# A two-layer residual block: rounding of the down weights on ScalarE and their later store, mask construction in batch 1's half, and other PSUM banks for the last pair

## The reference

```python
g = jnp.einsum('bsd,edf->ebsf', h, Wg)
u = jnp.einsum('bsd,edf->ebsf', h, Wu)
expert_outs = jnp.einsum('ebsf,efd->ebsd', jax.nn.silu(g) * u, Wd)
...
masked_scores = jnp.where(mask, scores[:, None, :], NEG_INF)
pooled = jnp.einsum('bjl,bld->bjd', softmax(masked_scores), hidden) / cnt[..., None]
```

## Time and profile before

| | us |
|---|---|
| runs | 1126.43, 1127.67, 1129.34; median 1127.67 |
| profiled execution | 1127.99 |
| its span, first to last instruction | 1126.1 |
| granted TensorE clock, mean | 0.995 |
| busy: PE, DVE, ACT, POOL | 1104.9, 919.6, 709.4, 696.5 |

### The profile page before, as it was taken

The page is one execution under the profiler, slowest core; times in us unless marked ns, Lnnn a source line. Parts: engine busy times, 40 slices in busy tenths (PEclk is TensorE's granted clock), DMA queues, the critical chain, the costliest instruction groups (busy, mean ns, idle before and its releaser), DMA issues. The chain is left out here.

```text
span 1126.1 us, 16076 instructions
## 1 busy us (share of the span) xinstructions
PE 1104.9 (98%) x4856; PEld 903.9 (80%) x4856; DVE 919.6 (82%) x1218; ACT 709.4 (63%) x1268; POOL 696.5 (62%) x666
## 2 busy tenths in 40 slices
PE   8799999999999999999999999999999999999988
PEld 6577888778888888888878887888888888888866
DVE  6698777788877877787668899888888898888875
ACT  6475666566666666666556666666666666666663
POOL 7799999999987777778324444444444444444451
PEclk9899999999999999999999999999999999999999
DMA  6666665487666666666545555555555555555512
GB/s 218 251 259 233 249 231 212 177 306 283 235 259 262 261 237 235 239 233 255 218 173 203 179 198 182 203 204 203 206 206 206 206 206 205 206 205 206 203 41 75
DMA packets 66484, 241.24 MB, mean 214 GB/s; under 512 B 6496, under 2 KB 38752, under 8 KB 57184
## 3 DMA queue, kind: packets, MB, share of 16 engines
q1 hardware_dynamic: 65584, 239.70, 57.6%
q10 hardware_dynamic: 816, 0.52, 0.2%
HBM read 134.29 MB, written 105.91 MB: 213 GB/s over the span
## 5 line engine op out<-in xcount | busy, mean ns | idle before, releaser
L811 ACT ACTIVATE silu<-g_ps 128x512 f32<-128x512 f32 x144 | 86.3, 599 | 180.1 <-PE g_ps L1480 180.1
L1478 PE MATMUL v_both<-xs_hi,wq 128*128 128x512 f32 x432 | 170.0, 393 | 3.3 <-DVE up L1146 2.6
L1479 PE MATMUL v_both<-xs_hi,wq 128*128 128x512 f32 x432 | 168.6, 390 | 0.0
L1480 PE MATMUL v_both<-xs_lo,wq 128*128 128x512 f32 x432 | 168.5, 390 | 0.0
L1141 DVE TENSOR_TENSOR gate<-e_ps,v_part 128x512 f32<-128x512 f32 x144 | 99.0, 687 | 66.4 <-PE e_ps L1480 66.2
L805 ACT ACTIVATE v_both<-g_ps 128x512 f32<-128x512 f32 x144 | 83.9, 583 | 101.7 <-PE g_ps L1480 101.4
L711 POOL TENSOR_TENSOR a<-a,a_own 128x512 f32<-128x512 f32 x35 | 56.1, 1604 | 137.4 <-DVE a_own L1173 137.4
L708 POOL TENSOR_TENSOR s<-a_own,a 128x512 f32<-128x512 f32 x35 | 56.3, 1610 | 131.0 <-DVE a_own L1192 131.0
L1478 PE MATMUL g_ps<-xs_hi,wq 128*128 128x512 f32 x288 | 113.0, 392 | 9.5 <-ACT v_both L805 9.5
L817 ACT ACTIVATE p_sb<-e_ps 128x512 f32<-128x512 f32 x144 | 86.2, 598 | 48.4 <-PE e_ps L1480 47.5
L1478 PE MATMUL e_ps<-xs_hi,wq 128*128 128x512 f32 x288 | 112.7, 391 | 0.4 <-ACT p_sb L817 0.4
(11 more groups left out here) (233 smaller groups left out, 2883.5 us busy)
## 6 DMA issues: line engine op xcount, KB each, us to landing
wq_kept<-wq SPq DMA_DIRECT2D x72, 896.0 KB, 5.5
wq<-wq_kept SPq DMA_DIRECT2D x72, 896.0 KB, 4.5
wd_kept<-wd SPq DMA_DIRECT2D x36, 1024.0 KB, 5.4
wd<-wd_kept SPq DMA_DIRECT2D x36, 1024.0 KB, 6.1
raw_d<-in_L_cond_Wd SPq DMA_DIRECT2D x32, 256.0 KB, 3.1
raw<-in_L_cond_Wg SPq DMA_DIRECT2D x31, 256.0 KB, 2.7
raw<-in_L_cond_Wu SPq DMA_DIRECT2D x31, 256.0 KB, 3.5
out_x<-x SPq DMA_DIRECT2D x8, 256.0 KB, 2.1
```

Source lines behind the costliest of these rows:

```text
L811: nc.scalar.activation(silu0[:, i % 2, :], g_ps[:], ACT.Silu).then_inc(silu0_done, 1)
L1478: nc.tensor.matmul(ps, w_hi, a_hi, start=start, stop=False, skip_group_check=True)
L1479: nc.tensor.matmul(ps, w_lo, a_hi, start=False, stop=False, skip_group_check=True)
L1480: return nc.tensor.matmul(ps, w_hi, a_lo, start=False, stop=stop, skip_group_check=True)
```

## The change

Eight things change in the code. (1) ScalarE gets `round_d(k)` at the end of even groups and `round_td(k)` at the end of odd ones, each one 128x512 copy; POOL keeps the lo parts (`rest_d`, `rest_td`) and `sums_d`, and of the old `split_d` only pair 0. (2) `raw_d` has three slots; SP loads pair 2 at n = 1. (3) `keep_d(k)`, the wait for `td_split`, the load of pair k+3 and the store of pair k, is moved from use 2k+1 to use 2k+6, so the last three lie in batch 1. (4) POOL makes the constants and masks in eleven parts, behind `sums_h(1)` to `sums_h(11)`. (5) `L1_AT` goes from 74 to 104; `add_acc(1)` of batch 0 stays at 74. (6) The last pair adds into `LAST`: `g_ps` and `v_ps[0]` for token half 0, `acc[0][1]` and `e_ps` for half 1; its first quarter stands ahead of `turn_sum(143)`. (7) VectorE's group 143 is written anew (`last_odd`), s3's drain goes to `p7_sb`, one of POOL's joins goes to VectorE. (8) ScalarE copies a11 to `res` ahead of `gate_second(143)`; batch 1's `attn` writes `acc[0][0]`.

```diff
+    RAWD = 3
...
+    KEEP = 3
...
-        raw_d = place("raw_d", [P, RAWS, DN, P], F32, work_at + 8 * BANK * 4)
+        raw_d = [place(f"raw_d{n}", [P, DN, P], F32, work_at + at * BANK * 4) for n, at in enumerate((8, 10, 25))]
...
-        L1_AT = end_of_b[0] + LAG + 1
+        ADD_AT = end_of_b[0] + LAG + 1
+        L1_AT = NU + 32
...
+        LAST = [[g_ps[:], v_ps[0]], [acc[0][1], e_ps[:]]]
+        ATT = [e_ps, acc[0][0]]
...
+            def keep_d(k):
+                sp.wait_ge(td_split, k + 1)
+                if k + RAWD < NU // PAIR:
+                    load_d(sp, k + RAWD)
+                sp.dma_start(wd_kept[k], wd[:, k % DR].bitcast(F32)).then_inc(wd_stored[k % DR], 16)
...
-                if n % PAIR == PAIR - 1:
-                    k = n // PAIR
-                    sp.wait_ge(td_split, k + 1)
-                    if m < NU // PAIR:
-                        load_d(sp, m)
-                    sp.dma_start(wd_kept[k], wd[:, k % DR].bitcast(F32)).then_inc(wd_stored[k % DR], 16)
+                if n == 1:
+                    load_d(sp, 2)
+                if n % PAIR == 0 and n // PAIR >= KEEP:
+                    keep_d(n // PAIR - KEEP)
...
+                k = i // PAIR - KEEP
+                if n % PAIR == 0 and k < NU // PAIR:
+                    keep_d(k)
...
             def split_d(n):
...
-                    pool.wait_ge(staged_d[s], (n // PAIR // RAWS + 1) * 16)
-                if n >= DR * PAIR:
-                    pool.wait_ge(down_done[1], n - DR * PAIR + 1)
-                    pool.wait_ge(wd_stored[n // PAIR % DR], n // PAIR // DR * 16)
-                k, own = n // PAIR % DR, slice(j * KD, (j + 1) * KD)
...
-                nc.gpsimd.tensor_tensor(hi, raw_d[:, s, own, :], zero[:, 0:1].unsqueeze(2).broadcast_to([P, KD, P]),
...
                                         ALU.add).then_inc(d_hi_done, 1)
                 pool.wait_ge(d_hi_done, n + 1)
-                nc.gpsimd.tensor_tensor(lo, raw_d[:, s, own, :], hi.bitcast(F32), ALU.subtract).then_inc(d_split, 1)
...
+            def rest_d(k):
+                own = slice(0, PAIR * KD)
+                pool.wait_ge(d_hi_done, PAIR + k)
+                nc.gpsimd.tensor_tensor(wd[:, k % DR, 1, own, :], raw_d[k % RAWD][:, own, :],
+                                        wd[:, k % DR, 0, own, :].bitcast(F32), ALU.subtract).then_inc(d_split, PAIR)
...
-                hi, lo = wd[:, k % DR, 0, 4:DN, :], wd[:, k % DR, 1, 4:DN, :]
-                nc.gpsimd.tensor_tensor(hi, w[:, 4:DN, :], zero[:, 0:1].unsqueeze(2).broadcast_to([P, DN - 4, P]),
-                                        ALU.add).then_inc(td_hi_done, 1)
+            def rest_td(k):
                 pool.wait_ge(td_hi_done, k + 1)
-                nc.gpsimd.tensor_tensor(lo, w[:, 4:DN, :], hi.bitcast(F32), ALU.subtract).then_inc(td_split, 1)
+                nc.gpsimd.tensor_tensor(wd[:, k % DR, 1, 4:DN, :], raw_d[k % RAWD][:, 4:DN, :],
+                                        wd[:, k % DR, 0, 4:DN, :].bitcast(F32), ALU.subtract).then_inc(td_split, 1)
...
-            EXTRA = {13: constants, 17: flags, 21: lambda: masks(0), 25: lambda: masks(1)}
...
-                if n in EXTRA:
-                    EXTRA[n]()
...
-                split_d(n)
+                if n < PAIR:
+                    split_d(n)
...
-                if n == 3:
-                    sums_d(0)
-                if n % PAIR and n > 1:
-                    sums_d(n // PAIR)
...
+                k = n // PAIR - 1
+                if n % PAIR == 0:
+                    if k >= 1:
+                        rest_d(k)
+                    if k >= 1:
+                        rest_td(k - 1)
+                elif k >= 0:
+                    sums_d(k)
+            last = NU // PAIR - 1
+            rest_d(last)
+            rest_td(last - 1)
+            sums_d(last)
+            rest_td(last)
...
                 joined_to(1, 0, xT[:, 1, 1, BANK:2 * BANK])
+                pool.wait_ge(res_step, 1)
+                joined_to(1, 0, res[:])
                 pool.wait_ge(res_step, 2)
-                joined_to(1, 0, res[:])
-                pool.wait_ge(res_step, 3)
-                joined_to(0, 1, res[:])
-                joined_to(1, 1, res[:])
+                joined_to(1, 1, p7_sb[:])
...
                     for p in range(SPS):
                         sums_h(p)
+                        if p in range(1, 12):
+                            pool.wait_ge(sum_made["s4"], p + 1)
+                        if p == 1:
+                            edges()
+                        elif p == 2:
+                            lanes()
+                        elif p == 3:
+                            blanks()
+                        elif p == 4:
...
+                        elif p in (6, 9):
+                            mask_of(p // 8)
+                        elif p in (7, 10):
+                            block_masks(p // 8)
+                        elif p in (8, 11):
+                            mask_ends(p // 11)
...
+            def round_d(k):
+                act.wait_ge(staged_d[k % RAWD], (k // RAWD + 1) * 16)
+                if k >= DR:
+                    act.wait_ge(down_done[1], (k - DR + 1) * PAIR)
+                    act.wait_ge(wd_stored[k % DR], k // DR * 16)
...
+                nc.scalar.activation(wd[:, k % DR, 0, own, :], raw_d[k % RAWD][:, own, :], ACT.Copy).then_inc(d_hi_done, 1)
+            def round_td(k):
+                act.wait_ge(td_step, 3 * (k + 1))
+                nc.scalar.activation(wd[:, k % DR, 0, 4:DN, :], raw_d[k % RAWD][:, 4:DN, :],
+                                     ACT.Copy).then_inc(td_hi_done, 1)
...
                     round_x(1, q)
+                if i % PAIR:
+                    round_td(i // PAIR)
+                elif i:
+                    round_d(i // PAIR)
...
                 if i + 1 < NG:
                     seed(i + 1)
-                gate_second(i)
                 if p == SPS:
                     act.wait_ge(c_used["a11"], SPS)
                     nc.scalar.activation(res[:], P_BANK["a11"], ACT.Copy).then_inc(p1_kept, 1)
+                gate_second(i)
...
-                    dve.wait_ge(joined, 2 * NT)
+                    dve.wait_ge(joined, 3)
+                    dve.wait_ge(res_step, 4)
...
                 for d in range(KD):
-                    nc.vector.tensor_tensor(xT[:, b, d, half], acc[d][t][:], xT[:, b, d, half],
+                    nc.vector.tensor_tensor(xT[:, b, d, half], LAST[t][d] if b else acc[d][t][:], xT[:, b, d, half],
...
-                if i == L1_AT:
+                if i == ADD_AT:
...
-                if p < SPS:
-                    rest_c("s3", p)
-                else:
-                    dve.wait_ge(p1_kept, 1)
-                    c11 = xT[:, 1, 0, 0:BANK]
-                    nc.vector.tensor_tensor(c11, P_BANK["a11"], c11, ALU.add).then_inc(res_step, 1)
-                    dve.wait_ge(c_used["s2"], SPS)
-                    nc.vector.tensor_tensor(res[:], P_BANK["s2"], res[:], ALU.add).then_inc(res_step, 1)
...
-                if p == SPS:
-                    dve.wait_ge(joined, NT)
-                    dve.wait_ge(res_step, 2)
-                    nc.vector.tensor_tensor(res[:], P_BANK["s3"], res[:], ALU.add).then_inc(res_step, 1)
...
+            def last_odd(i, p):
+                second_gate(i)
+                second_up(i)
+                hidden_second(i)
+                empty(i - 1)
+                dve.wait_ge(p1_kept, 1)
+                dve.wait_ge(c_used["s2"], SPS)
+                nc.vector.tensor_tensor(res[:], P_BANK["s2"], res[:], ALU.add).then_inc(res_step, 1)
+                hidden_first(i)
+                dve.wait_ge(c_used["s3"], SPS)
+                dve.wait_ge(res_step, 1)
+                nc.vector.tensor_tensor(p7_sb[:], P_BANK["s3"], res[:], ALU.add).then_inc(res_step, 1)
+                rest_c("a22", p)
+                rest_c("a12", p)
+                c11, c21 = xT[:, 1, 0, 0:BANK], xT[:, 1, 0, BANK:2 * BANK]
+                dve.wait_ge(c_used["a11"], SPS)
+                nc.vector.tensor_tensor(c11, P_BANK["a11"], c11, ALU.add).then_inc(res_step, 1)
+                dve.wait_ge(res_step, 2)
+                nc.vector.tensor_tensor(c21, c21, p7_sb[:], ALU.add).then_inc(res_step, 1)
+                dve.wait_ge(joined, 2)
+                empty(LAST_TURN)
+            for p in range(SPS):
                 even(NU + p * PAIR, p)
                 odd(NU + p * PAIR + 1, p)
-            empty(LAST_TURN)
+            even(NG - PAIR, SPS)
+            last_odd(NG - 1, SPS)
...
-            def last_pair():
...
-                        q = (("a11", "s3"), ("a12", "a22"))[f][t]
-                        if f == 0:
-                            pe.wait_ge(res_step, (3, 2)[t])
-                            down_sum(("a12", "a22")[t], SPS - 1, acc[0][t][:], True, False)
-                            if t:
-                                pe.wait_ge(emptied, LAST_TURN - FIRST_TURN + 1)
...
```

(73 more changed lines are left out.)

19 lines of the change are left out of this document (13 added, 6 removed).

## The result

| | before | after |
|---|---|---|
| median of 4 runs each, us | 1128.20 | 1118.28 |
| their range, us | 1126.43 to 1129.34 | 1117.90 to 1119.05 |
| ratio, 95% interval | | 0.9914, 0.9897 to 0.9931 |
| profiled execution / its span, us | 1127.99 / 1126.1 | 1118.34 / 1116.6 |

The change takes 9.9 us off the median, where 14.3 were forecast: faster by more than 0.3%, and inside the range by 0.3 us only, near its upper end. The kernel after is 4.6 us slower than the forecast's 1113.7, and the question of the experiments is where these went.

A forecast was written before the change was run, and what follows sets the result against it. TensorE was taken as the bound, with only its standing time to win. From 1127.99 us: -9.7 + 0 - 2.4 + 0.8 - 3.0 = -14.3, giving 1113.7 us; range 1109.8 to 1118.6.

The forecast's parts named there:

- The first hole: TensorE's pause at 38.53 to 46.70 us and the low clock behind it; SP's earlier store closes it, -9.7 us.
- the 1.4 of the term: Late `up`s in groups 5, 6 and 8 of batch 0; taken as 0, between -1.4 and +1.4 us.
- rival C: First hole only changes its owner, ScalarE being held as long in groups 1 to 4: 1123.4 or 1127 us; chance 0.10.
- The second hole: TensorE's waits behind masks(1) in batch 0, from about 204 us; they go when the masks leave, -2.4 us.
- ScalarE's and POOL's work in batch 0: ScalarE's added rounding copies fit its idle time and POOL only loses instructions; cost 0.
- 0.63 fits: 0: ScalarE's 0.63 us copy per group fits the 0.98 us idle ahead of the seed in batch 0; cost 0.
- rival A: VectorE's SBUF instructions collide with POOL's masks in eleven pairs of batch 1, 1.0 us a pair: 1123.9 us; chance 0.05.
- Masks in batch 1: Eleven mask parts behind s4 mostly fit POOL's idle time; the two mask_of make s3 late, +0.8 us.
- Rival B: POOL becomes the bound in batch 1, s3 and the seed late in eleven pairs: 1137 us, slower than before; chance 0.03.
- The end: Earlier up(143) and no wait ahead of the last pair, about 1090 us: -3.0 us.
- the masks' bound of 5.5 us: Upper bound for the masks in batch 1: eleven parts at 0.5 us each, in place of 0.8; sets the range's high end.

The follow-up runs named there:

- e4: Kernel before with only SP's new order (third raw_d slot, later keep_d): 1128.07 us, ratio 1.0000.
- e3: Kernel after with the rounding of the down weights (hi parts) given back from ScalarE to POOL: 1115.05 us, ratio 0.9881.
- e5: Kernel before with only the masks and constants moved to batch 1 and the second layer's steps at groups 104 to 118: 1126.35 us, ratio 0.9983.
- e1: Kernel after with one added wait: POOL starts rest_d only when VectorE has finished its rest_w: 1111.12 us, ratio 0.9846.
- e7: e1 with each of ScalarE's rounding copies made twice, the first into a spare tile: 1111.54 us, ratio 0.9855.
- e10: e1 run once more unchanged, for comparison on one chip with a version with split masks: 1110.86 us, ratio 0.9844.
- e6: Kernel before with only the new end (other banks, last_odd, first quarter ahead of the last turn): 1124.88 us, ratio 0.9972.
- e2: Kernel after with ScalarE's round_d and round_td moved into the next group, between gate_second and gate_first: 1117.81 us, ratio 0.9905.

## Why the prediction was right, and where it was not

**The first hole, -9.7: right.** Its gap and its low clock are gone, and after is 9.60 us ahead at group 5 and 9.98 at group 12; late `up`s of 0.38, 0.52 and 0.50 us stay in groups 3, 6 and 8, within the 1.4 of the term. But the prediction gave this gain to SP's order, and e4 shows that SP's order alone gives it back: rival C (the hole only changes owner) is what it does alone. What keeps the gain is not mainly ScalarE's rounding: e3, in which POOL rounds, still is 7.41 us ahead at groups 12 to 24, with the masks in batch 1 and POOL's steps in their new order. What each of these two does for the first groups, and ScalarE's rounding without SP's order, was not tried.

**The second hole, -2.4: right.** e5 measures 2.75. Before lost another 0.7 us in small places up to group 72, as e1 beside it shows, so 3.4 us came here.

**ScalarE's and POOL's work in batch 0, 0: the step that failed.** In the prediction: "0.63 fits: 0", and for POOL only what it loses. The first half is right, by e7. What was left out is that moving the hi part moves the *release* of POOL's lo part, from POOL's own order to the end of ScalarE's `round_d`, a fixed moment of each pair. There VectorE's `rest_w` begins. The loss is 6.99 us in 30 pairs (groups 12 to 72, after against e1), and one wait removes it. Before had such meetings too, 21 of its 59 `rest_w` between 100 and 540 us above 1.5 us, but the longest took 1.94.

That is rival A's mechanism in another half of the kernel. A had it in batch 1, where VectorE is busier but POOL's masks fall into idle places; there it cost nothing measurable. In batch 0 VectorE is busy 344.17 of 440 us, by this row of after (stretch, its length, then busy us and count of PE, PEld, DVE, ACT, POOL):

```profile
100.00:540.00 440.00, 439.93 (x1913) 356.53 (x1912) 344.17 (x407) 302.03 (x522) 265.48 (x230) 1.00 0.65 241
```

Almost 100 us of idle time did not help, since `rest_w` stands right ahead of `up`, and `up` has 0.85 us to spare (the 0.92 of the collision less the 0.07 by which p3 then starts late). Before's longest, 1.94 - 1.08 = 0.86, all but fits in that. I had weighed A by how full the engine is, and should have by what stands behind the slow instruction. The same row shows PE busy for 439.93 of 440: the loss is invisible in busy time and only shows in the count, 1913 matmuls against 1943 in the same stretch of e1 (30 x 0.227 = 6.8 us).

The timelines above also fit the rule of the Trainium skill (SBUF — State Buffer, "Who interferes with whom"), by which a VectorE instruction with two SBUF inputs and a GpSimd instruction that reads SBUF keep each other out for a whole instruction: `rest_d` ends at 237.04, and 1.08 us, the length of `rest_w` alone in e1, from there is 238.12; it ended at 237.99. POOL's next one, a 128x512 instruction like `rest_d`'s 1.29, took 2.15. The fit is not exact: both `rest_w` here and `hidden_first` in e1 (235.29 + 0.75 = 236.04 by the rule, 235.84 in the trace) ended 0.1 to 0.2 us sooner. `up`, one input of which is in PSUM, was 0.68 and 0.69 us in both kernels.

**Masks in batch 1, +0.8: right in place and size for e1, e5 and e10**, two waits of 0.35 us at the two `mask_of`. In after they don't show, and batch 1 gains 0.25 up to group 126 instead: there POOL's part took 4.3 us (663.20 to 667.51), in e1 5.2 (654.88 to 660.11). That its instructions are longer or shorter by what VectorE does beside them is how I read it. Rival B had no case. **The end, -3.0: right**, 2.8 (after and e6): `up(143)` is still late, by 0.27 from start to start, and two gaps of 0.15 and 0.36 follow; the 2.36 us are gone.

Summed over after's profile: -10.0 by group 12, -3.4 and +7.0 in the rest of batch 0, -0.25 in batch 1, -2.85 at the end: -9.5, the difference of the spans. So one term was wrong by 7.0 us and three came out 0.3, 1.0 and 1.05 us better than forecast (the end 0.15 less), which hid a part of it. That the time still lies inside the range is luck: the upper end was made of the masks' bound of 5.5 us, and the masks cost nothing in after, while the range held nothing for the term that failed. (By its own working the lower end is 1127.99 - 17.3 - 1 = 1109.7, not 1109.8. And the slow rows of rival A, 1180 ns on average, lie beside POOL's s3 and s1, not s1 and s2. Neither bears on the result.) The parts do not add up one by one: e4, e5 and e6 alone give 0.1, 2.4 and 3.9, together 6.4 of 9.9, and with the one wait 17.1.

Open: why rounding on ScalarE helps at the start (e3 is 2.6 us behind after at group 12) was only read from the waits for `up`, not tried apart. And e2's other places for `round_d` were not tried, nor another order of POOL's five instructions.

## What to carry to other kernels

When half of a job moves to another engine, ask what now releases the half that stays, and what the other engines do at that moment: in a steady loop a collision that came now and then becomes one in every period, always of the same length. Price it by the slack of the instruction right behind the slowed one, not by the engine's idle share; and look for it by counting matmuls in a stretch or by the period from start to start, since waits of 0.1 us stand in no wait list. Before crediting a queue order with a hole, ask which engine used that hole to catch up, and make the edit alone.

## What was not expected of the hardware

- A VectorE subtraction of 128x896 with both inputs in SBUF takes 1.08 us alone and 2.00 to 2.03 when a GpSimd instruction started 0.22 to 0.24 us ahead of it; GpSimd's 128x512 subtraction that comes behind goes from 1.29 to 2.15. Where VectorE's started first (228.51 in after) it took 1.14, and GpSimd's 1.47 in place of 0.74.
- After a wait too short for the list the second matmul's start is 0.34 us behind the first (238.65 to 238.99) instead of 0.227: a stall costs some 0.1 us beyond itself.
